# The transposes of an expert stage, done as quarter-tile products in halves

## The reference

```python
gate_logits = x @ gate_w + gate_b                      # x: normalized tokens, 64 wide
topk_vals, topk_idx = jax.lax.top_k(gate_logits, 2)
topk_w = jax.nn.softmax(topk_vals, axis=-1)
h = jax.nn.relu(jnp.einsum('bsh,ehf->bsef', x, w1) + b1)
expert_out = jnp.einsum('bsef,efh->bseh', h, w2) + b2
sel = jnp.take_along_axis(expert_out, topk_idx[:, :, :, None], axis=2)
moe = jnp.sum(topk_w[..., None] * sel, axis=2)
y = x + moe
mu, var = jnp.mean(y, axis=-1, keepdims=True), jnp.var(y, axis=-1, keepdims=True)
out = (y - mu) / jnp.sqrt(var + EPS) * gamma + beta    # added to the layer's input
```

## Time and profile before

| | before |
|---|---|
| median of 3 runs | 781.77 us (781.49 to 782.96) |
| the profiled execution | 780.84 us |
| its span, first to last instruction | 778.6 us |
| TensorE busy | 742.9 us, 95% |
| DVE, ACT, POOL busy | 81%, 68%, 59% |
| quarter products `up` / `down` busy | 147.0 / 148.7 us |
| transposes busy: gate weights, tokens, folds | 10.3, 10.3, 9.8 us |

### The profile page before, as it was taken

The page is one execution under the profiler, slowest core; times in us unless marked ns, Lnnn a source line. Parts: engine busy times, 40 slices in busy tenths (PEclk is TensorE's granted clock), DMA queues, the critical chain, the costliest instruction groups (busy, mean ns, idle before and its releaser), DMA issues.

```text
span 778.6 us, 16797 instructions
## 1 busy us (share of the span) xinstructions
PE 742.9 (95%) x5712; PEld 431.7 (55%) x5712; DVE 630.1 (81%) x1534; ACT 533.1 (68%) x1053; POOL 457.0 (59%) x620
## 2 busy tenths in 40 slices
PE   2999999999999999999999999999999999999994
PEld 1444356666667666666666666544555555454441
DVE  8676778888888888888888887788888888888864
ACT  1566779888888889888898888554554655555441
POOL 7644324544446454554546442367788788888885
PEclk9999999999999999999999999999999999999997
DMA  6200202211221112211221112000000000000000
GB/s 195 86 3 1 56 1 55 46 35 31 56 56 29 41 42 55 56 28 38 47 56 41 34 38 54 2 2 1 9 12 12 8 8 8 9 16 7 9 7 21
DMA packets 22620, 25.47 MB, mean 33 GB/s; under 512 B 12520, under 2 KB 21480, under 8 KB 22408
## 3 DMA queue, kind: packets, MB, share of 16 engines
q1 hardware_dynamic: 21544, 23.14, 12.7%
q10 hardware_dynamic: 992, 1.26, 0.6%
HBM read 5.06 MB, written 2.43 MB: 10 GB/s over the span
## 4 chain that ended last, share of the span: by engine, by line
PE 69%; POOL 10%; DVE 8%; ACT 5%; issue 4%; DMA 2%; SPq 0%; ACTq 0%; POOLq 0%; DVEq 0%
PE bank L1391 14%; PE bank L1369 13%; PE bank L1264 9%; PE bank L1222 8%; PE bank L1135 5%; PE bank L1288 5%; PE bank L1290 4%; DVE m L855 3%; POOL xn L429 2%; POOL inv L420 2%; PE bank L1125 2%; ACT prob L624 2%; POOL inv L412 1%; DVE prob L901 1%; ACT sq L588 1%
## 5 line engine op out<-in xcount | busy, mean ns | idle before, releaser
L440 POOL TENSOR_TENSOR sq<-sq 125x256 f32<-125x256 f32 x128 | 97.4, 772 | 162.2 <-ACT sq L588 139.5
L901 DVE TENSOR_SCALAR prob<-prob,cap_hi,cap_lo 125x500 f32<-125x500 f32 x256 | 156.1, 636 | 41.2 <-ACT prob L624 39.7
L624 ACT ACTIVATE prob<-bank 125x500 f32<-125x500 f32 x256 | 148.2, 591 | 34.9 <-PE bank L1290 32.5
L1369 PE MATMUL bank<-cs,w_sb 64*64 64x500 f32 x1024 | 147.0, 580 | 2.2 <-DVE gated L1019 2.0
L1391 PE MATMUL bank<-gated,w_sb 64*64 64x500 f32 x1024 | 148.7, 588 | 0.0
L482 POOL TENSOR_TENSOR gated<-relu,wb 128x500 f32<-128x500 f32 x96 | 119.9, 1250 | 48.2 <-ACT relu L722 45.7
L1019 DVE SCALAR_TENSOR_TENSOR gated<-bank,nb,wb 128x500 f32<-128x500 f32 x160 | 114.9, 727 | 35.2 <-PE bank L1369 35.2
L722 ACT ACTIVATE relu<-bank,b_sb 128x500 f32<-128x500 f32 x96 | 64.6, 673 | 93.2 <-PE bank L1369 93.2
L1369 PEld LDWEIGHTS bank<-cs,w_sb 64*64 64x64 f32 x1024 | 53.1, 133 | 54.7 <-issue 48.1
L1222 PE MATMUL bank<-wqku_hi,s 128*125 128x512 f32 x192 | 78.2, 407 | 2.8 <-DVE s L836 1.2
L588 ACT ACTIVATE sq<-bank 125x512 f32<-125x512 f32 x128 | 75.2, 598 | 8.2 <-PE bank L1222 4.7
(11 more groups left out here) (188 smaller groups left out, 1569.0 us busy)
## 6 DMA issues: line engine op xcount, KB each, us to landing
m1e<-m1e SPq DMA_DIRECT2D x64, 125.0 KB, 2.3
m1o<-m1o SPq DMA_DIRECT2D x64, 125.0 KB, 2.3
out<-res SPq DMA_DIRECT2D x15, 125.0 KB
w_sb<-in_w SPq DMA_DIRECT2D x1, 1024.0 KB
xa<-xparts SPq DMA_DIRECT2D x3, 281.2 KB
w_sb<-in_w SPq DMA_DIRECT2D x1, 512.0 KB
xw<-xparts SPq DMA_DIRECT2D x3, 140.6 KB
xparts<-x_part SPq DMA_DIRECT2D x3, 125.0 KB, 3.2
```

What stands on the lines that cost most here:

```text
L440: gp.tensor_tensor(sq2[q][:, :, :], sq[q][:, :, 0:D // 2], sq[q][:, :, D // 2:D], ALU.add)\
L624: act.activation(prob[v % PROBS][:, :, c, :], bank[5 + n % 3][0:T, 0:C].rearrange("p (h l) -> p h l", h=2), ACT.Exp).then_inc(b_exp, 1)
L901: dve.tensor_scalar(part, part, cap_hi[0:T, h:h + 1], cap_lo[0:T, h:h + 1], ALU.min, ALU.max)\
L1369: last = pe.matmul(up_bank(g)[cols, 0:C], w1_sb[rows, g, cols], cs1[q % 3][rows, :], start=True, stop=True)
```

## The change

- The three transposes leave the full array. Each is now 16 products of 64 x 64 by 64 columns (61 for the last rows of a chunk) with a part of the identity as the moving operand, in two rounds: round `r = 0` reads the LO rows, `r = 1` the HI rows. A new semaphore per transpose (`c_xth`, `c_wth`, `c_fh`) makes the second round wait for the first.
- `down` is split into a HI and a LO call. `side_work` places chunk 0 of round 0 ahead of the HI call, the other three chunks between the two calls, and round 1 behind the LO call. `c_dn` counts at the end of the LO call.
- The tokens' transpose goes from slot 3 to slot 4 (with ACT's copy `tokens_c`), the fold from slot 6 to slot 5; the gate weights stay in slot 6. The last fold stays a full-array transpose.
- On ACT, `normed` writes one copy instead of two and is split: chunks 0 and 1 in slot 2, chunks 2 and 3 in slot 3 behind the y copies (it was in slot 1). `y_high` is copied before `y_low`.

```diff
-            def normed(q):
-
-                act.wait_ge(c_inv, 3 * q + 3)
-                wait(act, c_xt, q)
-                wait(act, c_half, q - 3)
-                for c in range(CH):
-                    last = act.activation(cxn[q % 4][:, c, :, :], h_all[:, q * CH + c, :].unsqueeze(1).to_broadcast([T, 2, D]),
+            def normed(q, chunks=range(CH), copies=2):
...
+                for c in chunks:
+                    last = act.activation(cxn[q % 4][:, c, 0:copies, :],
+                                          h_all[:, q * CH + c, :].unsqueeze(1).to_broadcast([T, copies, D]),
                                           ACT.Identity, bias=cnb[:, 0, c:c + 1], scale=cinv[:, 0, c:c + 1])
...
             def slot_c(p, v):
                 q = p - 1
+                if v == 2 and valid(p + 1):
+                    normed(p + 1, range(0, 2), 1)
                 if v == 3 and valid(p - 2):
                     act.wait_ge(c_dn, 8 * (p - 2) + 8)
                     wait(act, c_y, p - 2)
-                    act.activation(y_low[:, :], bank[0][:, 0:C], ACT.Copy).then_inc(c_yl, 1)
                     if p - 2 < PAIRS - 1:
                         act.activation(y_high[:, :], bank[1][:, 0:C], ACT.Copy).then_inc(c_yh, 1)
+                    act.activation(y_low[:, :], bank[0][:, 0:C], ACT.Copy).then_inc(c_yl, 1)
+                if v == 3 and valid(p + 1):
+                    normed(p + 1, range(2, CH), 1)
...
-                if v == 1 and valid(p + 1):
-                    normed(p + 1)
+                if v == 4 and valid(p + 1):
+                    tokens_c(p + 1)
...
-            def down(q, v):
-
-                if v == 0 and q == 0:
-                    pe.wait_ge(b_res, PAIRS)
-                for g in (2 * v, 2 * v + 1):
-                    wait_gated(pe, q, g)
-                for rows, y, copied in ((LO, bank[0], c_yl), (HI, bank[1], c_yh)):
-                    if v == 0:
-                        wait(pe, copied, q)
...
+            def down(q, v, rows):
+
+                y, copied = (bank[0], c_yl) if rows is LO else (bank[1], c_yh)
+                if rows is HI:
...
+                    for g in (2 * v, 2 * v + 1):
+                        wait_gated(pe, q, g)
+                if v == 0:
+                    wait(pe, copied, q)
+                for g, cols in ((2 * v, LO), (2 * v + 1, HI)):
+                    last = pe.matmul(y[cols, 0:C], w2_sb[rows, g, :], gated[g % 8][rows, :],
+                                     start=v == 0, stop=v == 7, skip_group_check=True)
+                if rows is LO:
+                    last.then_inc(c_dn, 1)
...
+            def tokens_part(q, r, c):
+                if c == 0 and r == 0:
+                    pe.wait_ge(c_hn, q + 1)
+                    wait(pe, c_yt, q - 3)
+                if c == 0 and r == 1:
+                    pe.wait_ge(c_xth, q - 1)
+                t = HALVES[r]
+                for cols in (LO, HI):
+                    last = pe.matmul(bank[2][cols, c * T + t.start:c * T + t.stop], cxn[q % 4][t, c, 0, :], ident[t, t],
+                                     start=True, stop=True)
+                if c == CH - 1:
+                    last.then_inc((c_xth, c_xt)[r], 1)
...
+            def fold_part(q, r, c):
+                if c == 0 and r == 0:
+                    pe.wait_ge(c_y, q + 1)
+                    pe.wait_ge(c_s1, min(q + 4, PAIRS))
+                if c == 0 and r == 1:
+                    pe.wait_ge(c_fh, q + 1)
+                rows = (LO, HI)[r]
+                for t in HALVES:
+                    last = pe.matmul(bank[2][t, c * 128 + rows.start:c * 128 + rows.stop],
+                                     y_moe[rows, c * T + t.start:c * T + t.stop], ident[rows, rows], start=True, stop=True)
...
+            def side_work(p, v, r, chunks):
+
+                for c in chunks:
+                    if v == 4 and valid(p + 1):
+                        tokens_part(p + 1, r, c)
+                    if v == 5 and 0 <= p - 2 < PAIRS - 1:
+                        fold_part(p - 2, r, c)
+                    if v == 6 and valid(p):
+                        weights_part(p, r, c)
...
+                q, n = (p - 2, v + 5) if v < 3 else (p - 1, v - 3)
+                side_work(p, v, 0, range(1))
+                if valid(q):
+                    down(q, n, HI)
+                side_work(p, v, 0, range(1, CH))
+                if valid(q):
+                    down(q, n, LO)
+                side_work(p, v, 1, range(CH))
```

More of the change, by code:

```diff
@@ L723, in slot_c @@
                             .then_inc(c_relu, 1)
-                if v == 1 and valid(p + 1):
-                    normed(p + 1)
+                if v == 4 and valid(p + 1):
+                    tokens_c(p + 1)
                 if v == 5 and 0 <= p - 3 < PAIRS - 1:
                     result(p - 3)
-                if v == 3 and valid(p + 1):
-                    tokens_c(p + 1)
                 if v == 6 and valid(p):
@@ L1379, in extra @@
                                   skip_group_check=True)
-            def down(q, v):
-                if v == 0 and q == 0:
-                    pe.wait_ge(b_res, PAIRS)
-                for g in (2 * v, 2 * v + 1):
-                    wait_gated(pe, q, g)
-                for rows, y, copied in ((LO, bank[0], c_yl), (HI, bank[1], c_yh)):
-                    if v == 0:
-                        wait(pe, copied, q)
-                    for g, cols in ((2 * v, LO), (2 * v + 1, HI)):
-                        last = pe.matmul(y[cols, 0:C], w2_sb[rows, g, :], gated[g % 8][rows, :],
-                                         start=v == 0, stop=v == 7, skip_group_check=True)
-                last.then_inc(c_dn, 1)
+            def down(q, v, rows):
+                y, copied = (bank[0], c_yl) if rows is LO else (bank[1], c_yh)
+                if rows is HI:
+                    if v == 0 and q == 0:
+                        pe.wait_ge(b_res, PAIRS)
+                    for g in (2 * v, 2 * v + 1):
[7 more added lines that the diff above has]
+                    last.then_inc(c_dn, 1)
             def logits(p):
@@ L1425, in fold_c, with weights_part @@
                 last.then_inc(c_f, 1)
+            HALVES = (slice(0, 64), slice(64, T))
+            def tokens_part(q, r, c):
[10 more added lines that the diff above has]
+                    last.then_inc((c_xth, c_xt)[r], 1)
+            def weights_part(p, r, c):
+                if c == 0 and r == 0:
+                    pe.wait_ge(c_gate, gate_count(p, GATE))
+                    wait(pe, c_wbs, p)
+                if c == 0 and r == 1:
+                    pe.wait_ge(c_wth, p)
+                t = HALVES[r]
+                rows = wtok[t, c, :, :].rearrange("p e r -> p (e r)")
+                for cols in (LO, HI):
+                    last = pe.matmul(bank[3][cols, c * T + t.start:c * T + t.stop], rows[:, cols], ident[t, t],
+                                     start=True, stop=True)
+                if c == CH - 1:
+                    last.then_inc((c_wth, c_wt)[r], 1)
+            def fold_part(q, r, c):
+                if c == 0 and r == 0:
+                    pe.wait_ge(c_y, q + 1)
+                    pe.wait_ge(c_s1, min(q + 4, PAIRS))
+                if c == 0 and r == 1:
+                    pe.wait_ge(c_fh, q + 1)
[3 more added lines that the diff above has]
+                                     y_moe[rows, c * T + t.start:c * T + t.stop], ident[rows, rows], start=True, stop=True)
+                if c == CH - 1:
+                    last.then_inc((c_fh, c_f)[r], 1)
+            def side_work(p, v, r, chunks):
[6 more added lines that the diff above has]
+                        weights_part(p, r, c)
             def slot_c(p, v):
@@ L1433, in slot_c @@
                     logits(p)
-                if v == 3:
-                    if valid(p + 1):
-                        tokens_c(p + 1)
-                if v == 6:
-                    if valid(p):
-                        weights_c(p)
-                    if valid(p - 2):
-                        fold_c(p - 2)
-                if v < 3 and valid(p - 2):
-                    down(p - 2, v + 5)
-                if v >= 3 and valid(p - 1):
-                    down(p - 1, v - 3)
+                q, n = (p - 2, v + 5) if v < 3 else (p - 1, v - 3)
[6 more added lines that the diff above has]
+                side_work(p, v, 1, range(CH))
+                if v == 5 and p - 2 == PAIRS - 1:
+                    fold_c(p - 2)
                 if v == 3 and valid(p - 1):
```

8 lines of the change are left out of this document (7 added, 1 removed).

## The result

| | before | after |
|---|---|---|
| median of the runs | 782.29 us | 807.57 us (806.64 to 808.99) |
| after / before, 95% interval | | 1.0315 [1.0301, 1.033] |
| span of the profiled execution | 778.6 us | 804.5 us |
| TensorE, one `logits` to the next | 16.54 us | 18.34 us |

The forecast was 776.0, with a range up to 786.0: wrong in sign, and outside the range. Thirteen periods of 1.80 us more are 23.4 of the 25.3 us; the rest lies in the periods at either end. The mean granted clock is 0.994, against 0.995 before, so the clock is no part of it.

The account below looks back on a forecast made before the run. TensorE was taken to bound the kernel. The period was 16.54 - 2.27 + 1.29 + 0.52 + 0.08 + 0.04 = 16.20 us; the saving over 13 periods plus about 0.9 us at the ends gave 776.0 us, range 771.5 to 786.

Parts of the forecast that it names:

- three full-array transposes gone: TensorE's tokens, fold and gate-weight transposes need both row halves empty; removing them saves 2.27 us a period.
- 24 passes: One row half's new transpose products, 8 passes for each of three transposes at 0.054 us, add 1.29 us a period.
- y copies: Slot 3's `down` waits for ACT to copy out y_high and y_low, formerly hidden by the token transposes; 0.52 us a period.
- second half waits for the first: A transpose's second round waits for its first, on the upper half; slack and the 0.84 us `down` cover it: nothing.
- ACT, POOL and tokens' copy: Later cnb from POOL, partly offset by narrower `normed` on ACT, 0.08 us; fold in slot 5 waiting for tokens' copy, 0.04.
- The price of a pass: Each 64-column pass of the new TensorE products costs 0.054 us, weight load hidden; upper bound 0.112.
- the rival with uncovered loads: Weight loads stay exposed, a pass costs 0.112 us, period 17.60, 796 us; chance 0.10.
- the first rival: In slots 4 to 6 lower-half products start only 0.42 us after the upper `down`; 0.93 a period, about 789 us; chance 0.14.
- the other new waits: Second half of each transpose waiting for its first, on the upper half; covered by slack and `down`, cost nothing.
- a product at 623.60 ahead of one at 623.74: Trace row where an `up` pair starts before a b2 pair ahead of it in the program; taken as halves running independently.
- a floor (15.92, by its 0.62 of idle time): DVE waits 0.62 us for TensorE before its last group, so the period can fall no lower than 15.92.
- a period pays one half's share three times: Both row halves do equal extra transpose work at once, so three shares of 0.43 us, 1.29 a period, are paid.

Follow-up runs that it names:

- `d_r0first`: The changed kernel with all eight products of each transpose's first round ahead of the upper `down`, none between the two downs; 804.11 us, ratio 1.0278.
- `r6`: `r2` with `normed` split again, the tokens' first round at the end of slot 3 and every 500-column POOL product in two halves; 785.83 us, ratio 1.0038.
- `r2`: The changed kernel with second rounds one slot later, `normed` whole in slot 1, weights' copy in slot 7, y_moe before POOL's gate product 6; 783.54 us, 1.0013.
- `b_split`: The kernel before the change with every 500-column POOL product cut into two halves of 250 columns, nothing else; 786.58 us, ratio 1.005.

## Why the prediction was wrong

The period by the forecast's own terms, with what was measured:

| term | forecast | measured |
|---|---|---|
| three full-array transposes gone | -2.27 | -2.27 (none left in the period) |
| 24 passes | +1.29 | +1.53 (0.51 a round that waited) |
| y copies | +0.52 | +0.62 |
| second half waits for the first | nothing | +0.99 (3 x 0.33) |
| `up` of slot 5 waits for DVE | not there | +1.03 |
| ACT, POOL and tokens' copy | +0.12 | not seen; DVE's wait hides them |
| period from 16.54 | 16.20 | 18.44 by the sum, 18.34 by the trace |

The sum comes out 0.10 too long, probably because the waits stand on the upper half, which doesn't do `logits`.

**Right.** The price of a pass: 0.054 taken, 0.058 measured, loads hidden, but for the first pass of a round that had to wait (0.10); the rival with uncovered loads is out. The start of a lower-half product does run past an upper-half product: the first round goes beside the upper `down` in one stretch (618.38, 14 of its 16 passes), with no second clump 0.4 later, so the first rival's mechanism is out as well, though its price of 0.93 happens to be near the 0.99 of another one. The y copies were the forecast's largest new cost and came out at that size: slot 3 takes 2.72 (614.72 to 617.44) where 2.62 was worked out, with y_low as releaser.

**The first step that failed** is the sentence on "the other new waits", of which it said that "the `down` of 0.84 covers them: nothing". It counted when the first round's products are done, by its own passes, and not when their semaphore can come. The row that the forecast rested on, a product at 623.60 ahead of one at 623.74, is a row on starts; nothing in it says that semaphores overtake too. They don't. The second round starts 0.16 after the end of the `down` that stands ahead of the first round's last products (change), and its first load 0.09 after the first round's own end where no such `down` is ahead (`d_r0first`). The Trainium skill ("TensorE: Matmul & The Clock Gate", section "Part 3: Packing small matmuls — row/col tiling") says that matmuls keep the program's order in start and in end. The forecast set the whole sentence aside for the starts; the half of it on ends holds here for when a semaphore comes, by those 0.16 and 0.09.

**The second step that failed** is the one that wasn't there: DVE was costed only as a floor (15.92, by its 0.62 of idle time), with the durations that it had before. Its durations are not its own: a router step takes 0.22, or as long as POOL's running product lasts. The forecast moved `normed` and with it POOL's gate products by 0.73, worked out when `cnb` and y_moe would come, and didn't ask on which DVE steps the products would then fall. The row that shows the price, 1.17 us for a step beside y_moe, was in the trace of before. The Trainium skill ("SBUF — State Buffer", section "🔬 SBUF: two separate sides") states that DVE and GpSimd have a pair of ports in common that one instruction holds for its whole length, and that a DVE operation with two SBUF inputs needs it. This case's rows agree: the long steps in the change read two tiles (lg and top, lg and desc) and end 0.08 after POOL's product, while the step with one input at 620.04 takes 0.22 and the group that reads a PSUM bank at 620.18 takes 0.73, beside the next POOL product as alone.

**What held, and why it doesn't pay.** The forecast said that "both halves then do the same amount of extra work at once, so a period pays one half's share three times". In the change the upper half pays that share with the wait in front of it, 0.33 + 0.51 a transpose, 2.52 for three: more than the 2.27 that were removed. With that wait designed away (`r6`) the lower half pays 1.44, so 0.83 of the 2.27 is gained, where the forecast had 0.98. But waits on the same half take more than that back: 0.54 for the y copies, which the tokens' old place hid (0.49 of waiting, and a `down` that runs 0.05 longer behind it), 0.19 for group 7's bank and 0.22 for the copy of the gate weights, 0.95 in all. So `r6` ends at 16.76, above the 16.54 of before. In `r2`, which at 1.0013 comes closest to the kernel before, the loop through DVE, POOL and ACT takes the gain; how much each wait in it costs wasn't added up.

Open: how far a start may run past the other half. In the change the upper `down` passes one chunk (two products) of the first round that stands ahead of it in the program: it starts at 618.33, they at 618.38. Eight products ahead held a start up: in `d_r0first` the upper `down` began 0.25 after the first of them, in `r6` the first pass of `up` in slot 4 0.35 after (610.28 against 609.93), with its own rows free in both. Nothing between was run. The change without any order between its two rounds wasn't tried, since both write the same bank.

## What to carry to other kernels

When an edit shifts when POOL works, lay its instructions over DVE's in the trace and look for one DVE operation that is short in one place and as long as a POOL instruction in another: that row is the price of a collision, and a shift of 0.7 us can multiply it. In this kernel a semaphore on a matmul came only when the other half's product ahead of it in the program had ended, so a wait between row halves is costed from the last product ahead of the signal, not from the signalling product's own end. And before crediting a removed barrier, list the waits that its time covered: here they came to 0.95 us a period in `r6`, against 0.83 gained.

## What the chip did that I had not expected

- A DVE step of 0.22 us took 0.94, 1.17 and 1.28 beside POOL products of 1.25, each to 0.08 after POOL's end; beside halves it took 0.64 and 0.75. POOL seems to be held in its turn: its `yz` product, 0.74 in `b_split`, took 1.23 in the change (at 622.21), where DVE's wtok step of 0.68 had started 0.04 before it. No run was made for that.
- Matmul starts of different row halves overtake, their semaphores don't: the load that waited for one came 0.49 after the signalling product's recorded end and 0.16 after that of the other half's product ahead of it.
- Eight products of one half ahead of the other half's product held it up for 0.25 (`d_r0first`) and 0.35 us (`r6`) from the first of them, though its rows were free; two didn't.
